# Fused four-layer cross-attention on one core: mean squares kept in PSUM, the last layer's bias in pieces, row maxima in another order and one unit earlier

## The chip, the cores and the metric

The kernel runs on 1 core of one Trainium2 chip. The time is device microseconds of one execution, the median of several runs. Lower is better. Engines: PE is TensorE, DVE is VectorE, ACT is ScalarE, POOL is GpSimd, SP issues the DMAs.

## The reference, cut to what matters

Four attention layers are applied in a row to `x` (4 batches x 512 tokens x 256 channels), each against the same context (4 x 1024 keys x 512 channels). Layers 0, 2 and 3 have 16 heads of 64 and add a bias of -20 on two or four key columns of masked tokens. Layer 1 normalizes `x` first (RMS norm) and has 16 query heads of 16 that share 4 key heads.

```python
# layers 0, 2, 3
q, k, v = x @ Wq, ctx @ Wk, ctx @ Wv                  # 16 heads of 64
logits = q k^T * 64**-0.5 + col_bias                  # 512 x 1024 per head
x = softmax(logits) v @ Wo + bo + x
# layer 1
inv = rsqrt(mean(x*x, axis=-1) + 1e-5); xn = x * inv * norm_w
q, k, v = xn @ wq, ctx @ wk, ctx @ wv                 # 16 query heads, 4 key heads, of 16
x = x + softmax(q k^T * 16**-0.5) v @ wo
```

## The kernel before, in words

**Items.** A wide layer is worked through as 32 items: 8 pairs of heads, and 4 batches for each. Layer 1 is 16 items: 4 groups of four heads, and 4 batches. So there are N = 112 items, numbered `p`; layer 1's are 32 to 47 (`G0` = 32, `G1` = 48), layer 2 starts at 48, layer 3 at 80. The kernel is a pipeline over slots `s`. In slot `s` PE computes the scores of item `s` (4 score blocks of two key tiles each), the row maxima of item `s+1`, the projections of keys and queries of item `s+2` and of values of `s+1`, and the second half of attention, the sums and the output projection of item `s-1`. Every engine has its instructions in an order written out by hand (`wide_slot`, `first_group_slot`, `group_slot`), the same sequence of names for all engines; semaphores with constants tie them together. f32 operands are split into two f16 halves, high and low (`k_h`, `k_l` and so on), and multiplied in three passes (`products`, L613).

**Row maxima.** `maxima(p, u)` has 8 units for a wide item: `t` is a block of 128 tokens, `half` a half of the 1024 keys. PE writes 2 heads x 512 scores to `ps_sm` (L684), which is a single buffer, and DVE adds the bias and takes the minimum of the negated sums in two custom instructions (L1293) with a read of the accumulator after each. A unit of the second half starts from the result of the first half (`nmx` is an operand), a unit of the first half from a constant. Two units go with each score block: one leads it and one trails it. Before the unit that trails, PE must wait until DVE is done with the one that leads. When all 8 units are done, ACT spreads the maxima (`columns_of_maxima`, L1037), PE transposes them (`rows_of_maxima`, L693) and DVE writes them to `ext_q` (`extra_rows`, L1314), from which PE adds them to the scores (L719).

**Two banks in turn.** Everything else that PE makes goes to `ps_j`, two banks used in turn in the order of `bank_users()`. `take` makes PE wait until the bank's last user has been read.

**RMS norm.** For the 4 batches (slots 30 to 33, `rms_batch`): ACT squares `x`, PE averages over channels with a matrix of 1/256 (`mean_squares`, L782), ACT copies the result to `v_rms` and takes exp(-0.5 ln), DVE refines it by one Newton step and multiplies `x` by it (`normed`, L1339 to L1344), POOL splits the product in `xh` and `xl` (`split_x`, L474 and L475), and PE projects the queries of layer 1 at the end of the slot (`late_queries`).

**Bias.** `bias_m` (4 token blocks x 1024 keys) holds the bias that DVE adds to the maxima. Eight matmuls (L790), one per token block and half, make it, each copied by ACT (L1065). Layer 3's are made in a row at the end of slot 78.

**Other names.** `second_half` (L1321) adds the two halves of attention in `o_un`; `sums_out` (ACT, L1016) and `reciprocal` (DVE, L1326, two of 256 columns) turn the row sums around; `normalize` (POOL, L523) multiplies; `output_hi` (ACT, L1044) and `output_lo` (POOL, L528) split the result for the output projection; POOL's `add` (L509) sums the exponentials over key tiles for the row sums.

## Time and profile before

| | |
|---|---|
| median of 3 runs | 3739.59 us (3733.17 to 3739.71) |
| the profiled execution | 3736.15 us, its span 3734.4 us |
| mean granted TensorE clock | 0.986 of full speed |
| PE busy | 3534.4 us, 95% |
| DVE, POOL, ACT busy | 66%, 54%, 46% |
| DMA | 39.44 MB, 11 GB/s over the span |

PE is busy nearly all the time. A slot of a wide layer takes 31.56 us in the middle of a layer; from 1027 to 1188 us, around the change to layer 1, slots are longer and the granted clock is lower. A row of the timeline reads: start, duration, engine, line, operation, output and inputs, shape, how many in a row, and in brackets how long the engine was idle before it and who ended that. Idle time matters where it is PE's.

### The profile page before, as it was taken

The page shows a single profiled execution, that of the slowest core. Times are in us where ns is not written, and L with a number is a line of the kernel's source. Part 1 is how long each engine was busy: PE and PEld are TensorE (multiplying, and loading weights), DVE is VectorE, ACT ScalarE, POOL GpSimd, SP SyncE. Part 2 cuts the span into 40 slices and gives each one's busy share as a digit, 9 for nine tenths or more (in the row PEclk, how much of TensorE's full clock was granted, in tenths as well). Part 3 has the DMA queues.
Part 4 walks back from the last instruction along what each step waited for, and adds up shares of the span by engine and source line. Part 5 has one row for each costly group of instructions (what it writes and reads, how often), then busy time and mean ns, then how long its engine had stood idle before and what let it go on. Part 6 is the DMA issues. An engine that isn't in the chain of part 4 may idle for free. (4 is left out here: it accounts for less than half of the span.)

```text
span 3734.4 us, 69744 instructions
## 1 busy us (share of the span) xinstructions
PE 3534.4 (95%) x27496; PEld 1552.8 (42%) x27496; DVE 2469.8 (66%) x4487; ACT 1704.6 (46%) x2146; POOL 2005.6 (54%) x968
## 2 busy tenths in 40 slices
PE   5999999999987888989999999999999999999997
PEld 2444444444432222224444444444444444444443
DVE  6666666666666788875666666666566666666664
ACT  3444444444444666664444444444444444444443
POOL 5755566666551000026556666656775555556666
PEclk8999999999998999999999999999999999999999
DMA  3000000000000000000000000000000000000000
GB/s 135 10 10 10 1 9 10 10 1 8 8 4 8 1 8 9 1 9 10 10 1 10 10 10 1 10 10 8 3 10 10 1 10 10 10 1 10 3 1 23
DMA packets 47503, 39.44 MB, mean 11 GB/s; under 512 B 2768, under 2 KB 40784, under 8 KB 47184
## 3 DMA queue, kind: packets, MB, share of 16 engines
q1 hardware_dynamic: 47184, 34.99, 3.0%
q8 instruction: 225, 3.69, 0.4%
q14 instruction: 94, 0.77, 0.1%
HBM read 32.88 MB, written 2.10 MB: 9 GB/s over the span
## 5 line engine op out<-in xcount | busy, mean ns | idle before, releaser
L509 POOL TENSOR_TENSOR acc<-acc,pt 128x1024 f32<-128x1024 f32 x576 | 1380.7, 2397 | 211.7 <-ACT pt L1011 170.5
L1011 ACT ACTIVATE pt<-ps_st 128x1024 f32<-128x1024 f32 x768 | 744.6, 1021 | 602.5 <-PE ps_st L719 602.5
L523 POOL TENSOR_TENSOR o_un<-o_un,rinv 128x512 f32<-128x512 f32 x112 | 142.7, 1274 | 1227.3 <-DVE rinv L1326 1227.3
L1293 DVE CUSTOM_DVE_ANT_0 ps_sm<-ps_sm,bias_m 128x512 f32<-128x512 f32 x760 | 510.9, 714 | 370.3 <-PE ps_sm L684 370.2
L761 PE MATMUL ps_j<-pt,v 128*64 128x512 f32 x3072 | 704.7, 601 | 2.0 <-ACT pt L1011 2.0
L1293 DVE CUSTOM_DVE_ANT_0 ps_sm<-ps_sm,bias_m,nmx 128x512 f32<-128x512 f32 x760 | 543.3, 756 | 69.3 <-PE ps_sm L684 60.0
L613 PE MATMUL ps_j<-w_h,ctx_h 128*128 128x128 f16 x3072 | 529.4, 220 | 0.5 <-DVE x L1334 0.5
L613 PE MATMUL ps_j<-w_h,ctx_l 128*128 128x128 f16 x3072 | 527.4, 220 | 0.0
L613 PE MATMUL ps_j<-w_l,ctx_h 128*128 128x128 f16 x3072 | 527.4, 220 | 0.0
L1326 DVE RECIPROCAL rinv<-rinv 128x256 f32<-128x256 f32 x224 | 391.3, 1748 | 64.1 <-ACT rinv L1016 63.8
L613 PE MATMUL ps_j<-ctx_h,w_h 128*128 128x512 f16 x896 | 342.0, 382 | 46.4 <-DVE o_un L1321 14.7
L761 PEld LDWEIGHTS ps_j<-pt,v 128*64 128x64 f32 x3072 | 204.2, 137 | 397.8 <-issue 394.3
L684 PE MATMUL ps_sm<-k_h,q_h 64*128 64x512 f16 x1528 | 300.7, 385 | 54.8 <-DVE nmx L1293 54.8
L613 PE MATMUL ps_j<-ctx_h,w_l 128*128 128x512 f16 x896 | 341.7, 381 | 0.0
L613 PE MATMUL ps_j<-ctx_l,w_h 128*128 128x512 f16 x896 | 341.7, 381 | 0.0
L1011 ACT ACTIVATE pt<-ps_sm 128x1024 f32<-128x1024 f32 x256 | 261.8, 1023 | 154.7 <-PE ps_sm L735 154.6
L1283 DVE TENSOR_REDUCE nmg<-ps_st 128x2 f32<-128x1024 f32 x248 | 295.8, 1212 | 48.1 <-PE ps_st L684 47.9
L613 PEld LDWEIGHTS ps_j<-w_h,ctx_h 128*128 128x128 f16 x3072 | 301.2, 98 | 44.8 <-issue 43.2
L1201 DVE SCALAR_TENSOR_TENSOR k_l<-ps_j,k_h 128x512 f16<-128x512 f32 x192 | 132.0, 688 | 280.5 <-ACT k_h L974 280.4
L613 PEld LDWEIGHTS ps_j<-w_l,ctx_h 128*128 128x128 f16 x3072 | 301.8, 98 | 0.0
L613 PEld LDWEIGHTS ps_j<-w_h,ctx_l 128*128 128x128 f16 x3072 | 301.7, 98 | 0.0
L509 POOL TENSOR_TENSOR acc<-pt 128x1024 f32<-128x1024 f32 x96 | 226.0, 2354 | 130.9 <-ACT pt L1011 130.9
(135 smaller groups left out, 4943.1 us busy)
## 6 DMA issues: line engine op xcount, KB each, us to landing
w_raw<-wk SPq DMA_DIRECT2D x28, 256.0 KB, 2.8
pt<-ctx_t SPq DMA_DIRECT2D x6, 1024.0 KB, 7.6
w_raw<-wv SPq DMA_DIRECT2D x24, 256.0 KB, 3.6
wo_raw<-wo SPq DMA_DIRECT2D x28, 128.0 KB, 2.0
w_raw<-wq SPq DMA_DIRECT2D x24, 128.0 KB, 2.8
x<-x_t SPq DMA_DIRECT2D x4, 512.0 KB, 8.4
acc<-ctx_t SPq DMA_DIRECT2D x2, 1024.0 KB, 8.2
out_t<-x SPq DMA_DIRECT2D x4, 512.0 KB, 2.8
```

Of the source, the lines that this page charges most:

```text
L509: G.tensor_tensor(total, first, pt[:, n % RING, :], ALU.add).then_inc(s_acc, 1)
L523: G.tensor_tensor(o, o, rinv[:], ALU.mult).then_inc(s_o, 1)
L613: done = MM(dst, l, r, start=first and i == 0, stop=last and i == n - 1)
L684: last = MM(dst[:, h, :], queries_in(p, tile)[d, t * P:(t + 1) * P], k_h[d, r, half * HALF:(half + 1) * HALF], start=True, stop=True)
L761: last = MM(dst[h * HD:(h + 1) * HD, :], values_of(p)[:, kt, h * HD:(h + 1) * HD], pt[:, (units(p) + kt) % RING, h * TQ:(h + 1) * TQ], sta ...
L1011: A(pt[:, n % RING, :], src.rearrange("p h q -> p (h q)"), ACT.Exp).then_inc(s_exp, 1)
L1201: return V.scalar_tensor_tensor(dst, src, scale, hi, ALU.mult, ALU.subtract)
L1283: V.tensor_reduce(nmg[:, half, t, 2 * tile:2 * tile + 2], src, AX_X, ALU.max, negate=True).then_inc(s_max, 1)
L1293: last = V.tensor_tensor_reduce(out=src[:, h, :], in0=src[:, h, :], in1=bias_m[:, t, half * HALF:(half + 1) * HALF], scale=-1.0, scalar=nm ...
L1326: V.reciprocal(r, r).then_inc(s_rinv, 1)
```

## The change

1. **Order and place of the maxima.** The units of a wide item come in the order of `piece`: (token block, half) = (0,0) (1,0) (0,1) (2,0) (1,1) (3,0) (2,1) (3,1). The first unit of item `s+2` is taken at the last of slot `s`'s eight places, so that the other seven of item `s+1` stand at the first seven places (`passes`, where `early` allows: items 1 to 31 and 50 to 111).
2. **Maxima out earlier.** ACT spreads the maxima before the exponentials 6 and 7 of the slot, PE transposes them in the middle of the second projection of values, so `extra_rows` stands on DVE ahead of the next slot.
3. **RMS norm.** For the first two batches the mean squares stay in their bank of `ps_j` and DVE works on them there; the other users of that stretch (`pvb`, `sum`, `k0`) share the other bank. The Newton step has three instructions in place of four. `normed` stands ahead of both reciprocals; ACT makes `xh` (`normed_hi`), POOL only `xl` (`normed_lo`). In slots 32 and 33 all of it moves a few steps later.
4. **Bias of layer 3.** Its eight matmuls are spread over slot 78 and the start of slot 79, one ahead of and one behind each score block.

```diff
+def last_bias(s, gap, after):
+    if after and gap < 0:
+        s, gap = s - 1, 3
+    return 16 + 2 * gap + after if s == STARTS[3] - 2 else None
+def piece(u):
+    return ((0, 0), (1, 0), (0, 1), (2, 0), (1, 1), (3, 0), (2, 1), (3, 1))[u]
+def early(p):
+    return p < N and not any(grouped(q) for q in (p - 2, p - 1, p)) and p >= 1
+def passes(s):
+    places = [[] for _ in range(8)]
+    p = s + 1
+    if 0 <= p < N:
+        for i, u in enumerate(range(1 if early(p) else 0, 8)):
+            places[i].append((p, u))
+    if early(s + 2):
+        places[7].append((s + 2, 0))
+    return places
...
@@ bank_users
+            bias(-1, 1)
             if rms_batch(s) is not None:
-                then("ms", rms_batch(s))
...
+                then("ms", rms_batch(s), 0)
+                then("pvb", s - 1, 1)
+                then("sum", s - 1, 1)
+                then("k0", s + 2, 1)
...
@@ POOL
-                if layer == GROUPED:
-                    pool.wait_ge(s_xn, b + 1)
-                    src = sq[:]
...
+            def normed_lo(b):
+                pool.wait_ge(s_xn_h, b + 1)
+                pool.wait_ge(s_q, queries(G0 - B + b + 1))
+                G.tensor_tensor(of_batch(xl, b), sq[:], of_batch(xh, b), ALU.subtract).then_inc(s_xs, 1)
@@ PE, take
+                    elif before == "ms" and m < 2:
+                        pe.wait_ge(s_xn, m + 1)
...
@@ PE, wide_slot
                 def score_block(i):
+                    if i and last_bias(s, i - 1, 0) is not None:
+                        bias_matrix(last_bias(s, i - 1, 0))
                     peak()
                     if now:
                         scores(s, i)
                     peak()
+                    if last_bias(s, i - 1, 1) is not None:
+                        bias_matrix(last_bias(s, i - 1, 1))
...
-                if nxt and has_values(s + 1):
+                if nxt and not grouped(s + 1):
+                    project_v(s + 1, 1, range(0, 2))
+                    rows_of_maxima(s + 1, 0)
+                    project_v(s + 1, 1, range(2, 4))
...
@@ PE, first_group_slot and group_slot
                 maxima(s, 9)
-                mean_squares(rms_batch(s))
+                attend(s - 1, 1)
                 maxima(s, 10)
-                attend(s - 1, 1)
...
-                    if i == 0 and s == G0 + 1:
+                    if i == 0 and first:
                         mean_squares(rms_batch(s))
...
-                    if i in (5, 6):
-                        if first:
-                            project_out(s - 1, i - 5)
+                    if i in (7, 8) and first:
+                        project_out(s - 1, i - 7)
...
+                    if i == 15 and first:
+                        mean_squares(rms_batch(s + 1))
@@ ACT
-                A(v_rms[:], bank("ms", b), ACT.Identity, bias=flags[:, FLAG_EPS:FLAG_EPS + 1]).then_inc(s_ms_sb, 1)
...
+                if b >= 2:
+                    A(v_rms[:], bank("ms", b), ACT.Copy).then_inc(s_ms_sb, 1)
...
+            def normed_hi(b):
+                act.wait_ge(s_xn, b + 1)
+                act.wait_ge(s_q, queries(G0 - B + b + 1))
+                A(of_batch(xh, b), sq[:], ACT.Copy).then_inc(s_xn_h, 1)
...
                     first_half_out(s)
+                    bias(2, 0)
+                if nxt and not grouped(s + 1):
+                    columns_of_maxima(s + 1)
+                if now:
                     exponentials(s, 6)
                     exponentials(s, 7)
-                if nxt and not grouped(s + 1):
-                    columns_of_maxima(s + 1)
...
@@ DVE
             def normed(b):
...
-                link(V.tensor_tensor(t_rms, y_rms[:], y_rms[:], ALU.mult))
-                link(V.tensor_tensor(t_rms, t_rms, v_rms[:], ALU.mult))
-                link(V.tensor_scalar(t_rms, t_rms, -0.5, 1.5, ALU.mult, ALU.add))
-                link(V.tensor_tensor(y_rms[:], t_rms, y_rms[:], ALU.mult))
+                ms = means_of(b)
+                link(V.scalar_tensor_tensor(ms, ms, EPS, y_rms[:], ALU.add, ALU.mult))
+                link(V.scalar_tensor_tensor(ms, ms, -0.5, y_rms[:], ALU.mult, ALU.mult))
+                link(V.scalar_tensor_tensor(ms, ms, 1.5, y_rms[:], ALU.add, ALU.mult))
...
-                if past:
+                if rms_batch(s) is not None:
+                    normed(rms_batch(s))
+                elif past:
                     reciprocal(s - 1, 0)
...
@@ DVE, group_slot
+                    if i in (4, 5) and first:
+                        reciprocal(s - 1, i - 4)
+                    if i == 6 and rms_batch(s) is not None:
                         normed(rms_batch(s))
```

**Order on PE at the end of a slot of a wide layer.** The rows are PE's around the transposition of the maxima (`nm_w`); `w_h`, `w_l` with `ctx_h`, `ctx_l` are the second projection of values, of which only the last rows stand here; `ps_sm` is the leading unit of maxima of the next slot. Before:

```order
L613 MATMUL ps_j<-w_h,ctx_h 128x128
L613 MATMUL ps_j<-w_l,ctx_h 128x128
L613 MATMUL ps_j<-w_h,ctx_l 128x128
L693 MATMUL ps_j<-ident_sb,nm_w 128x128 [waits s_x,s_nm16]
L693 MATMUL ps_j<-ident_sb,nm_w 128x128 x3
L684 MATMUL ps_sm<-k_h,q_h 128x512 [waits s_max,s_q_h,s_k_h]
```

Now, at the same place:

```order
L663 MATMUL ps_j<-w_l,ctx_h 128x128
L663 MATMUL ps_j<-w_h,ctx_l 128x128
L747 MATMUL ps_j<-ident_sb,nm_w 128x128 [waits s_x,s_nm16]
L747 MATMUL ps_j<-ident_sb,nm_w 128x128 x3
L663 MATMUL ps_j<-w_h,ctx_h 128x128
L663 MATMUL ps_j<-w_l,ctx_h 128x128
```

The transposition has moved ahead of the last 24 of the 48 matmuls of the projection; after these follows the next slot's leading unit.

**Order on ACT at the same place.** `o_un` is the first half of attention, `pt` the exponentials, `nm_w` the spread maxima, `v` the values. Before:

```order
L1021 ACTIVATE o_un<-ps_j 128x512 [waits s_o_l,s_pva]
L1011 ACTIVATE pt<-ps_st 128x1024 [waits s_acc,s_pva,s_st] x2
L1037 ACTIVATE nm_w<-nmx 128x512 [waits s_max,s_nm]
L995 ACTIVATE v<-ps_j 128x512 [waits s_pvb,s_v]
L1011 ACTIVATE pt<-ps_st 128x1024 [waits s_acc,s_pva,s_st] x2
```

Now:

```order
L1082 ACTIVATE o_un<-ps_j 128x512 [waits s_o_l,s_pva]
L1098 ACTIVATE nm_w<-nmx 128x512 [waits s_max,s_nm]
L1072 ACTIVATE pt<-ps_st 128x1024 [waits s_acc,s_pva,s_st] x2
L1056 ACTIVATE v<-ps_j 128x512 [waits s_pvb,s_v]
L1072 ACTIVATE pt<-ps_st 128x1024 [waits s_acc,s_pva,s_st] x2
```

The spread of the maxima now stands ahead of the last two exponentials of the slot, and waits for the maxima while these are queued behind it.

**Order on DVE in slot 30, the first with an RMS norm.** `rinv` is the reciprocal of the sums, `k_h` the low part of layer 1's keys, `sq`, `v_rms`, `y_rms` belong to the norm. Before:

```order
L1326 RECIPROCAL rinv<-rinv 128x256 [waits s_sum_sb]
L1339 TENSOR_TENSOR sq<-y_rms 128x512 [waits s_ms,s_rsqrt]
L1340 TENSOR_TENSOR sq<-sq,v_rms 128x512 [waits s_dve]
L1341 TENSOR_SCALAR sq<-sq 128x512 [waits s_dve]
L1342 TENSOR_TENSOR y_rms<-sq,y_rms 128x512 [waits s_dve]
L1344 TENSOR_TENSOR sq<-x,y_rms 128x512 [waits s_dve]
L1344 TENSOR_TENSOR sq<-x,y_rms 128x512
L1201 SCALAR_TENSOR_TENSOR k_h<-ps_j,k_l 128x512 [waits s_k_h]
```

Now, the norm first, and the reciprocals behind two units of maxima:

```order
L1405 TENSOR_TENSOR o_un<-ps_j,o_un 128x512 [waits s_pva_sb,s_pvb]
L1425 SCALAR_TENSOR_TENSOR ps_j<-ps_j,y_rms 128x512 [waits s_ms,s_rsqrt]
L1426 SCALAR_TENSOR_TENSOR ps_j<-ps_j,y_rms 128x512 [waits s_dve]
L1427 SCALAR_TENSOR_TENSOR ps_j<-ps_j,y_rms 128x512 [waits s_dve]
L1429 TENSOR_TENSOR sq<-x,ps_j 128x512 [waits s_dve]
L1429 TENSOR_TENSOR sq<-x,ps_j 128x512
...
L1410 RECIPROCAL rinv<-rinv 128x256 [waits s_sum_sb] x2
L1285 SCALAR_TENSOR_TENSOR k_h<-ps_j,k_l 128x512 [waits s_k_h]
```

The norm has moved from behind the second reciprocal to ahead of the first, and both reciprocals stand in one piece between the maxima of score block 1 and the second half of the keys.

## Rows read from the trace of the kernel before

**Rows 1.** The page: busy time of PE, its share, instructions.
```profile
PE 3534.4 (95%) x27496; PEld 1552.8 (42%) x27496; DVE 2469.8 (66%) x4487; ACT 1704.6 (46%) x2146; POOL 2005.6 (54%) x968
```

**Rows 2.** PE's waits, whole span: us in total, times, longest.
```profile
PE ps_sm L684 <- DVE nmx L1293: 54.8, 101, 7.5
```

**Rows 3.** PE's waits from 1750 to 2500 us.
```profile
PE ps_sm L684 <- DVE nmx L1293: 7.3, 24, 0.3
```

**Rows 4.** Timeline of PE around the end of slot 60, columns as above.
```profile
2131.36 0.39 PE L684 MATMUL ps_sm<-k_h,q_h 64*128 64x512 f16 x2
...
2133.35 0.39 PE L684 MATMUL ps_sm<-k_h,q_h 64*128 64x512 f16 x2
...
2136.68 0.39 PE L684 MATMUL ps_sm<-k_h,q_h 64*128 64x512 f16 x2
...
2139.00 0.39 PE L684 MATMUL ps_sm<-k_h,q_h 64*128 64x512 f16 x2 [0.30 <-DVE nmx L1293]
```

**Rows 5.** Timeline of DVE in the same stretch.
```profile
2131.80 0.70 DVE L1293 CUSTOM_DVE_ANT_0 ps_sm<-ps_sm,bias_m 128x512 f32<-128x512 f32 x1 [3.38 <-PE ps_sm L684]
...
2133.06 0.14 DVE L1293 DVE_READ_ACCUMULATOR2_ANT nmx<- 128x1 f32 x1
...
2133.78 0.76 DVE L1293 CUSTOM_DVE_ANT_0 ps_sm<-ps_sm,bias_m,nmx 128x512 f32<-128x512 f32 x1
...
2135.13 0.14 DVE L1293 DVE_READ_ACCUMULATOR2_ANT nmx<- 128x1 f32 x1
2136.79 0.75 DVE L1314 SCALAR_TENSOR_TENSOR ext_q<-ps_j,flags_sb,bias_q 128x512 f16<-128x512 f32 x1 [1.52 <-PE ps_j L693]
...
2138.71 0.14 DVE L1293 DVE_READ_ACCUMULATOR2_ANT nmx<- 128x1 f32 x1
```

**Rows 6.** Timeline of ACT in the same stretch.
```profile
2133.42 1.94 ACT L1011 ACTIVATE pt<-ps_st 128x1024 f32<-128x1024 f32 x2 [2.10 <-PE ps_st L719]
2135.64 0.63 ACT L1037 ACTIVATE nm_w<-nmx 128x512 f16<-128x512 f32 x1 [0.28 <-issue]
```

**Rows 7.** Timeline of PE in slot 30.
```profile
1032.62 1.03 PE L774 MATMUL ps_j<-acc,ones_sb 128*64 128x512 f32 x4
...
1053.54 0.61 PE L684 MATMUL ps_sm<-k_h,q_h 64*128 64x512 f16 x2 [7.48 <-DVE nmx L1293]
```

**Rows 8.** Timeline of DVE in slot 30.
```profile
1032.84 0.69 DVE L1321 TENSOR_TENSOR o_un<-ps_j,o_un 128x512 f32<-128x512 f32 x1 [4.02 <-PE ps_j L761]
1034.34 1.75 DVE L1326 RECIPROCAL rinv<-rinv 128x256 f32<-128x256 f32 x1 [0.81 <-ACT rinv L1016]
...
1041.79 0.63 DVE L1339 TENSOR_TENSOR sq<-y_rms 128x512 f32<-128x512 f32 x1
...
1044.12 2.45 DVE L1341 TENSOR_SCALAR sq<-sq 128x512 f32<-128x512 f32 x1
...
1048.16 3.31 DVE L1344 TENSOR_TENSOR sq<-x,y_rms 128x512 f32<-128x512 f32 x2
```

**Rows 9.** Timeline of DVE in the first slot of layer 1.
```profile
1125.49 0.43 DVE L1341 TENSOR_SCALAR sq<-sq 128x512 f32<-128x512 f32 x1
...
1136.33 0.19 DVE L1302 TENSOR_REDUCE nmx<-nmg 128x16 f32<-128x32 f32 x1
```

**Rows 10.** Timeline of ACT in slot 30.
```profile
1043.57 0.63 ACT L1044 ACTIVATE o_h<-o_un 128x512 f16<-128x512 f32 x1 [1.41 <-POOL o_un L523]
1044.15 0.78 ACT L971 ACTIVATE k_l<-ps_j,flags_sb 128x512 f16<-128x512 f32 x1
```

**Rows 11.** Timeline of POOL in slot 30.
```profile
1043.50 2.79 POOL L509 TENSOR_TENSOR acc<-acc,pt 128x1024 f32<-128x1024 f32 x1
```

**Rows 12.** Window 1052 to 1061: busy us of each engine (instructions), PEclk, DMA.
```profile
1052.00:1061.00 9.00, 7.46 (x22) 2.00 (x23) 3.48 (x10) 0.00 (x0) 8.77 (x4) 0.60 0.01 2
```

**Rows 13.** Timeline of PE at the end of slot 78.
```profile
2674.05 0.38 PE L790 MATMUL ps_j<-ext_k,bias_q 32*128 32x512 f16 x1
...
2679.07 0.61 PE L693 MATMUL ps_j<-ident_sb,nm_w 128*128 128x128 f16 x4
```

More of the change, by code:

```diff
@@ L111, in owner @@
     return p, n - units(p)
-def first_of_wide(p):
-    return p in (STARTS[i] for i in WIDE)
 def rms_batch(s):
@@ L210, in bank_users @@
             then("out0", s - 1, 1)
+        else:
+            then("ms", rms_batch(s + 1), 1)
         if s == G1 - 1:
@@ L378, in queries_in, with means_of @@
             return (q_l if tile else q_h)[:, p % 3, :]
+        def means_of(b):
+            return bank("ms", b) if b < 2 else v_rms[:]
         def of_batch(t, b):
@@ L548, in _ @@
                     add(s, 1)
[L549 to L550 removed]
+                if s == G0 + 1:
+                    normed_lo(rms_batch(s))
                 if past:
@@ L558, in _ @@
                     add(s, 3)
-                if rms_batch(s) is not None and not grouped(s):
-                    split_x(GROUPED, rms_batch(s))
                 if summing:
-                    for kt in range(4, KT):
+                    add(s, 4)
+                if rms_batch(s) is not None and s <= G0:
+                    normed_lo(rms_batch(s))
+                if summing:
+                    for kt in range(5, KT):
                         add(s, kt)
@@ L646, in project_v @@
                     wh, wl = w_h[:, set_of(p) % 2, WV0:], w_l[:, set_of(p) % 2, WV0:]
-                dst = take(f"v{half}", p)
-                for k in range(4):
+                if 0 in tiles:
+                    take(f"v{half}", p)
+                dst = bank(f"v{half}", p)
+                for k in tiles:
                     kt = slice((half * 4 + k) * P, (half * 4 + k + 1) * P)
@@ L1073, in wide_slot, with bias @@
                 now, nxt, far, past = 0 <= s < N, 0 <= s + 1 < N, 0 <= s + 2 < N, 0 <= s - 1 < N
+                def bias(gap, after):
+                    if last_bias(s, gap, after) is not None:
+                        bias_out(last_bias(s, gap, after))
                 def context(*parts):
@@ L1285, in maxima @@
                     return
-                t, half = u // 2, u % 2
-                if u == 0:
-                    reaches(dve, s_nm16, p)
+                t, half = piece(u)
+                if u in (0, 2):
+                    reaches(dve, s_nm16, p if u else p - early(p))
                 if half:
-                    dve.wait_ge(s_max, units(p) + u)
+                    dve.wait_ge(s_max, units(p) + [piece(i) for i in range(8)].index((t, 0)) + 1)
                 dve.wait_ge(s_bias_sb, 8 * WIDE.index(layer_of(p)) + u + 1)
```

139 lines of the change are left out of this document (75 added, 64 removed).

## Prediction

> **What bounds the kernel.** I read the page first, then PE's waits, then timelines. PE is busy for 95% of the span [rows 1], so time can come only from PE's waits, from the lower clock, or from fewer matmuls; the change adds and removes no matmul. The reader is to see in [rows 2] that the largest wait is for DVE's part of a unit of row maxima: 54.8 us in 101 waits. In 750 us in the middle of layers 2 and 3 there are 24 such waits of 0.3 us [rows 3], and 750 us are 24 slots: one in every slot. The rest of the 54.8 us lies in a few long waits, one of 7.48 us in slot 30 [rows 7].
>
> **The wait in every slot.** In [rows 4] the unit that leads a score block starts at 2131.36 and the one that trails it at 2133.35, 1.99 us later, with no wait. At the start of the next slot it is 2136.68 to 2139.00, 2.32 us: 0.33 more. [Rows 5] show why. DVE does `extra_rows` from 2136.79, released by PE's transposition, and begins the leading unit behind it; the unit ends at 2138.85, and PE starts 0.15 us later. Now PE transposes in the middle of the projection of values, some 1.6 us earlier (24 of the 48 matmuls that fill most of 2133.67 to 2136.36), so DVE is done with `extra_rows` before the leading unit arrives. 0.33 us go.
>
> What is late next? A unit of the first half takes DVE from 2131.80 to 2133.20, 1.40 us, and with 0.15 us to PE this is just the 1.99 us at which PE comes anyway: 2133.35. A unit of the second half takes 2133.78 to 2135.27, 1.49 us [rows 5]. Before, every leading unit was of the first half. In the new order those of score blocks 0, 1 and 2 still are, but block 3 is led by (3,1): its trailing unit waits 0.09 us. Net 0.24 us a slot. The slots with the wait are 1 to 29, 49 to 77 and 80 to 110, 89 in all: **21.4 us**.
>
> Two moves need cover. ACT spreads the maxima (0.63 us) ahead of exponentials 6 and 7 [rows 6], which start at 2133.42; the maxima are there at 2133.29, so the pair ends 0.6 us later, near 2136.0. PE's next scores overwrite that buffer from 2136.9 on (0.3 earlier now): 0.5 us of cover or more. And the transposition needs the spread maxima, near 2134.2, while PE comes to it after 2135. If the cover were gone, PE would wait for ACT in each slot. Moving one unit to the slot before moves work, it adds none; only in slot 48, where the last place has two units, does PE wait for a whole unit of DVE: 1.49 + 0.15 and the start, **2.0 us lost**. In slot -1 it has two as well, but slot 0 waits for DVE afterwards, and that wait shrinks: I count 0.6 us won.
>
> **Slot 30.** Before, the norm takes DVE from 1041.79 to 1051.47, 9.7 us [rows 8], and the unit of maxima behind it makes PE wait 7.48 us, until 1053.54 [rows 7]. Five of its six instructions would take some 0.7 us: the first does (0.63). The ones beside POOL's additions take 2.45 and 3.31 (for two); the same L1341 takes 0.43 in slot 32, where POOL does nothing [rows 8, 9, 11]. I bound the new norm by 3.5 us (five instructions of 0.7) and by 9.7, and take 3.5, as POOL waits for the reciprocals while it runs.
>
> The Trainium skill (SBUF — State Buffer, "Who interferes with whom") says that a VectorE instruction with two SBUF inputs or in a two-port mode contends with GpSimd for a shared pair of ports, and one with at most one SBUF input does not. The 2.45 against 0.43 us agrees. By that rule the new chain, with the mean squares in PSUM, would take 3.5 us even beside an addition, and the bound of 9.7 would not be met; the sum is the same.
>
> The chain then, all times as if in the old trace. The halves are added at 1032.84 for 0.69 [rows 8], 0.33 earlier now, to 1033.2. `sum` shares that bank now and can only start 0.15 later, at 1033.35, where it could have started at 1032.3; then ACT must read it (0.6) before `k0`: in all `k0` starts at 1035.2 instead of 1033.35. The norm runs from 1033.2 to 1036.7, in the gap of DVE that this opens; the first unit of block 1 comes 2.7 us after the start of `k0` (twelve matmuls of 0.22), at 1037.9. So the norm is hidden. But the reciprocals now stand behind the maxima of block 1: DVE is free for them at 1041.75, two take 3.4, one 1.75 [rows 8], POOL multiplies (1.4), ACT makes `o_h` (0.63) and only then the keys' high half (0.78) [rows 10], DVE its low half (0.68) and the leading unit of block 2 (1.4): 1050.05, PE at 1050.2. So a wait of some 2.6 us is left in place of 7.48, and its end comes 3.3 us earlier. After the old wait PE's clock is low: 0.60 over 1052 to 1061, with 7.46 us of matmuls [rows 12], which at full speed are 4.5: 3.0 us more to gain if the clock stays up after the shorter wait. That can't be read here; I count half. With 0.6 for the maxima that left slot 30 and for a bank freed earlier: 3.3 + 0.6 + 1.5 = **5.4 us**. The low half `xl` is ready by 1057, before PE asks for it near 1060.
>
> **Slot 31** has the same order, but one more instruction of 0.7 ahead of the norm, and the reductions wait for the queries' low half first: I take 1.5 less, **3.9 us**.
>
> **Start of layer 1.** DVE is the chain there, up to the minimum over both halves at 1136.33 [rows 9]. The norm (3.9 with its reads, no POOL beside it), two reciprocals (3.5) and PE's mean squares (2.0) leave it: 9.1 us earlier, allowing 0.3 for overlap. In slot 32, however, reciprocals and norm return on DVE between units 4 and 7, where it is still the chain: 3.5 + 3.6 come back, less 2.2 us in which it had waited for PE: 4.9. In slot 33 the norm now stands ahead of keys that PE waits for: 1.0. Net **3.2 us**.
>
> **Bias of layer 3.** From its first matmul at 2674.05 to the transposition at 2679.07 are 5.0 us [rows 13], and the low clock behind it adds 2.0 in a slot of 38.6. Spread out, each matmul costs 0.22 (1.8 for eight) and waits for the bank before it. I find 0.2 to 0.3 us for those that wait for DVE's low halves, and about 1.2, 1.0 and 0.8 where the next user waits for ACT's copy behind two exponentials (`pva`, `nm0`) or for the values: 4.1. So 5.9 for 7.0: **1.1 us**.
>
> **Sum.** 21.4 - 2.0 + 0.6 + 5.4 + 3.9 + 3.2 + 1.1 = 33.6 us. The profiled execution took 3736.15, 3.4 below the median of the runs shown: 3702.5 by the one, 3706.0 by the other. I take **3704 us**, own range 3693 to 3715.
>
> **The rivals.**
>
> *A. The waits around layer 1 only move* (0.20). Clock low again after waits of 2.6 us; the norm and the reciprocals, later, cost in slots 32 and 33 what was won ahead of them. For it: PE's clock is already low there, and `o_h` ahead of the keys on ACT is a new queue. Against it: 9.7 us on DVE really become 3.5. It leaves 21.1 us and nothing from the norm: 3716 us.
>
> *B. The norm's gain is not given back* (0.17). The clock stays up in slots 30 and 31 (1.5 + 1.0), and DVE takes norm and reciprocals in slot 32 where PE isn't waiting (4.9) and 33 (1.0). 8.4 us more: 3696 us.
>
> *C. The wait in each slot finds another engine* (0.08). PE's 1.99 us are exactly DVE's 1.40 + 0.15 from the start of DVE, so there is no slack, and block 3 or the spread maxima may take up the 0.24. Against it: nothing else on DVE precedes the unit. 21.4 less: 3725 us.
>
> *D. ACT holds PE, slower than before* (0.03). If exponentials 6 and 7 come more than 0.5 us later than I have them, PE's next scores wait in all slots. 33.6 us over 89 slots are 0.38 a slot: from exponentials 0.9 us later than reckoned the kernel is slower. At the whole 0.63 a slot 56 us are lost: 3760 us. Against it: the maxima that ACT waits for are done 0.13 us before it is free.
>
> The forecast has 0.52. Shared out, the range of 8 in 10 is 3686 to 3722: it takes in A and B, and leaves out C and D. What a measurement can tell from no change here is 0.2%, 7.5 us. Faster by more: all but D and the tail of C: 0.94; within: 0.03; slower: 0.03.
>
> **What would show it.** In the new profile: no wait for `nmx` at the start of a slot, trailing units at 1.99 us in blocks 0 to 2 and at 2.08 in block 3, `nm_w` ahead of the exponentials, a slot near 31.3 us. In slot 30 the norm on DVE as five instructions near 0.7 us, a wait of PE for DVE of 2 to 3 us at block 2, the granted clock after it. In slot 32 reductions, reciprocals and norm without a gap on DVE. In slot 78 waits of PE at `pva` and at the transposition. Wrong would be: slots still of 31.5 us, PE waiting for ACT in ordinary slots, or a wait over 5 us in slots 30 and 31.

## The result and the profile after

The changed kernel takes **3688.49 us** (median of 4 runs, 3687.80 to 3690.56), the kernel before beside it 3736.38 (4 runs). The ratio is 0.9874, 95% interval 0.9857 to 0.9891: 47.9 us, or 1.3%, faster. The forecast was 3704 us, a gain of 33.6, with a range from 3686 to 3722. So direction and range held, and so did the mechanism of the largest term, but 14 us more came than the sum had, and the narrower range of 3693 to 3715 was missed. The profiled execution's span went from 3734.4 to 3686.0 us. One of the four executions of `dve_late` below took 10273.54 us at a granted clock of 0.333 and is left out of its figures.

On the page, PE's busy time is nearly what it was [rows 1]; the 48 us came out of its waits.

```profile
PE 3531.1 (96%) x27496; PEld 1554.9 (42%) x27496; DVE 2406.0 (65%) x4483; ACT 1696.2 (46%) x2148; POOL 1995.9 (54%) x964
```

PE's waits over the whole span, kernel after (total us, times, longest), answering to [rows 2]:

```profile
PE ps_sm L738 <- DVE nmx L1377: 23.0, 12, 5.7
...
PE ps_j L663 <- POOL o_l L574: 16.0, 4, 7.3
```

The same view of 1750 to 2500 us, answering to [rows 3], has one line left:

```profile
PE ps_j L663 <- DVE o_un L1405: 0.6, 1, 0.6
```

From 101 waits for the maxima 12 are left. But the reader should put a second row of before beside these. It was in the same answer as [rows 2], and the prediction passed it over:

```profile
PE ps_j L613 <- DVE o_un L1321: 14.7, 29, 1.2
```

After, waits of this kind are down to four (0.6 in slots 9 and 53 each, 0.9 in slots 30 and 31 each). These waits are most of what the forecast missed.

**An ordinary slot after** (end of a slot on PE; start us, us, then in brackets the idle time ahead and who ended it), answering to [rows 4]:

```profile
2096.39 0.39 PE L738 MATMUL ps_sm<-k_h,q_h 64*128 64x512 f16 x2
...
2098.46 0.39 PE L738 MATMUL ps_sm<-k_h,q_h 64*128 64x512 f16 x2
...
2100.14 0.39 PE L747 MATMUL ps_j<-ident_sb,nm_w 128*128 128x128 f16 x4
```

On DVE and ACT in the same stretch, answering to [rows 5, 6]:

```profile
2100.56 0.75 DVE L1398 SCALAR_TENSOR_TENSOR ext_q<-ps_j,flags_sb,bias_q 128x512 f16<-128x512 f32 x1 [0.26 <-PE ps_j L747]
2102.23 0.70 DVE L1377 CUSTOM_DVE_ANT_0 ps_sm<-ps_sm,bias_m 128x512 f32<-128x512 f32 x1 [0.92 <-PE ps_sm L738]
```
```profile
2098.41 0.63 ACT L1098 ACTIVATE nm_w<-nmx 128x512 f16<-128x512 f32 x1 [2.05 <-DVE nmx L1377]
2098.94 1.92 ACT L1072 ACTIVATE pt<-ps_st 128x1024 f32<-128x1024 f32 x2
```

`ext_q` is done at 2101.31, 0.92 us before DVE is handed the leading unit of the next slot: DVE now waits for PE there, and not PE for DVE. The trailing unit of block 3 comes 2.07 us after the leading one (2098.46 against 2096.39), as forecast (2.08). The maxima are spread ahead of the exponentials; ACT waits 2.05 us for them, as it waited 2.10 us for PE's scores there before [rows 6], and PE waits for nobody.

To compare slot by slot I take the time from a slot's first exponential on ACT to the next slot's; the last row ends with the last exponential, and what follows it took 19.1 us before and 20.2 after. The sums, us against the profiled execution of before (a minus is faster):

| Part | before | after, change | forecast |
|---|---|---|---|
| before slot 0, and slot 0 | 103.7 | -5.2 | -0.6 |
| slots 1-29 | 922.9 | -12.6 | -7.0 |
| slots 30-33 | 200.9 | -12.5 | -12.5 |
| slots 34-47 | 468.4 | -1.1 | 0 |
| slot 48 | 27.7 | +3.9 | +2.0 |
| slots 49-77 | 921.2 | -12.4 | -7.0 |
| slots 78, 79 | 70.1 | -1.3 | -1.1 |
| slots 80-109 | 948.7 | -9.3 | -7.2 |
| slots 110, 111 | 51.7 | +1.0 | -0.2 |

A plain slot went from 31.56 to 31.31 us, in every one of them: 0.25, forecast 0.24. What the forecast lacks lies in slots 5, 13, 17, 21 and so on, one in four, which went from 31.84 to 31.31, and in slots 9 to 12 and 53 to 56, from between 32.22 and 32.76 to 31.31 to 31.92. The first and the last row hold more than the change: executions of one order differ there. From slot 111's first exponential to the end of the span `before` took 41.2 us, and `norm_only` and `wo_late`, which have the old order too, 44.0, like the changed kernel.

### The profile page after: what moved, and what is told of

It reads as the page before. It is cut to its first block, busy times and chain, and to the rows that moved or that the text cites. A ratio compares the mean times of both kernels' runs of the same rounds, so it can differ in the third digit from the quotient of the medians.

```text
span 3686.0 us, 69837 instructions
## 1 busy us (share of the span) xinstructions
PE 3531.1 (96%) x27496; PEld 1554.9 (42%) x27496; DVE 2406.0 (65%) x4483; ACT 1696.2 (46%) x2148; POOL 1995.9 (54%) x964
## 4 chain that ended last, share of the span: by engine, by line
PE 90%; DVE 4%; issue 3%; ACT 2%; POOL 1%; DMA 0%; POOLq 0%; ACTq 0%; DVEq 0%
PE ps_j L663 39%; PE ps_j L815 18%; PE ps_st L767 13%; PE ps_sm L738 7%; PE ps_st L773 3%; PE ps_j L802 3%; PE ps_j L828 2%; PE ps_st L738 1%; PE ps_sm L789 1%; PE ps_j L747 1%; ACT pt L1072 1%; DVE nmg L1367 1%; ACT k_l L1032 1%; DVE k_h L1285 1%; DVE ps_sm L1377 0%
## 5 line engine op out<-in xcount | busy, mean ns | idle before, releaser
L767 PE MATMUL ps_st<-q_h,k_h 64*128 64x512 f16 x1536 | 291.4, 376 | 2.0 <-ACT pt L1072 2.0
```

Source lines behind the costliest of these rows:

```text
L767: MM(ps_st[:, side, h, :], k[d, r, keys], q[d, r, :], start=n == 0, stop=False)
```

## The experiments

All ratios are against the kernel before, run on the same chip.

**The small instruction ahead of o_un.** In one slot in four, DVE makes the low half of Wo (`wo_l`, 128x256) between the trailing unit and `o_un`. Slot 61 before, DVE and then POOL:

```profile
2108.93 2.62 DVE L1201 SCALAR_TENSOR_TENSOR wo_l<-wo_raw,wo_h 128x256 f16<-128x256 f32 x1
2111.47 0.68 DVE L1321 TENSOR_TENSOR o_un<-ps_j,o_un 128x512 f32<-128x512 f32 x1
```
```profile
2108.91 2.35 POOL L509 TENSOR_TENSOR acc<-pt 128x1024 f32<-128x1024 f32 x1 [1.39 <-ACT pt L1011]
```

Slot 5 after:

```profile
225.45 0.42 DVE L1285 SCALAR_TENSOR_TENSOR wo_l<-wo_raw,wo_h 128x256 f16<-128x256 f32 x1
227.69 0.69 DVE L1405 TENSOR_TENSOR o_un<-ps_j,o_un 128x512 f32<-128x512 f32 x1 [1.83 <-PE ps_j L815]
```
```profile
225.76 2.36 POOL L555 TENSOR_TENSOR acc<-pt 128x1024 f32<-128x1024 f32 x1 [1.00 <-ACT pt L1072]
```

Before, POOL's addition starts 0.02 us ahead of DVE's instruction, and this takes 2.62 us; after, DVE starts 0.31 us ahead of POOL, and it takes 0.42. The trailing unit used to be 0.33 us late while the exponential that releases POOL was not.

The token rows (slots 8 to 12 and 52 to 56) are a second case of it, at the same place on DVE. Slot 10, before and then after:

```profile
391.00 3.41 DVE L1252 SCALAR_TENSOR_TENSOR sq<-iota_sb,tok_f,sq 128x1024 f16<-128x1024 f16 x1
```
```profile
382.62 1.28 DVE L1336 SCALAR_TENSOR_TENSOR sq<-iota_sb,tok_f,sq 128x1024 f16<-128x1024 f16 x1
```

POOL's addition starts at 390.98 there, 0.02 us ahead, and at 382.93, 0.31 us behind. Two kernels test this.

The first, `dve_late`, is the changed kernel with POOL's start put ahead of DVE's again:

```diff
+                    dve.wait_ge(s_exp, units(s) + 2)
+                    V.tensor_copy(tok_f[:, 0, 0:1], tok_f[:, 0, 0:1])
                     wo_lo(set_of(s - 1))
```

> The changed kernel; ahead of the low half of Wo, DVE now waits for exponential 1 (the same event that releases POOL's first addition) and does one 128x1 copy, so that POOL's addition starts first. Nothing is moved or added otherwise. The theory (whoever starts first keeps the shared SBUF port for its whole instruction): the 128x256 instruction takes 2.6 us again instead of 0.42, o_un is late, and PE waits 0.6 to 0.7 us for it in 20 to 22 slots, as in slot 9 where one such case is left (0.64): 3688.5 + 14 = 3702 us. Rival (the instruction is faster for another reason than the order, for example because it has less to wait for from ACT): it stays at 0.42 to 0.5 us, DVE is ready 0.5 us before attend ends, and the time stays within 1 us of 3688.5.

Measured 3702.60 us (3 runs, 3700.56 to 3702.80; ratio 0.9920, 0.9903 to 0.9936): the gain of the change less 14.1 us. Its row of `wo_l` (min/median/max ns) and PE's wait, then slot 5:

```profile
L1285 DVE SCALAR_TENSOR_TENSOR wo_l<-wo_raw,wo_h x28: 411/2610/2617, 100.4 to 3594.2; 128x256 f16<-128x256 f32 x28
```
```profile
PE ps_j L663 <- DVE o_un L1405: 14.2, 21, 1.0
```
```profile
225.58 2.36 POOL L555 TENSOR_TENSOR acc<-pt 128x1024 f32<-128x1024 f32 x1 [0.99 <-ACT pt L1072]
```
```profile
225.61 2.61 DVE L1285 SCALAR_TENSOR_TENSOR wo_l<-wo_raw,wo_h 128x256 f16<-128x256 f32 x1
228.14 0.68 DVE L1405 TENSOR_TENSOR o_un<-ps_j,o_un 128x512 f32<-128x512 f32 x1
```

The same instruction, started 0.03 us behind POOL's and not 0.31 ahead, takes 2.2 us longer and ends 0.28 us after it. The start order decides. The copy and the wait cannot cost this by themselves: they start `wo_l` 0.16 us later, and in the changed kernel DVE had 1.83 us of idle time between `wo_l` and `o_un`. Nineteen slots went from 31.31 to 31.92, and 9 and 53 from 31.92 to 32.32. That is 0.61 us in a plain slot, where the same blocking cost 0.28 in the kernel before: PE was 0.33 us late there anyway. The token rows have no added wait in this kernel, still take 1.28 us in slot 10, and their slots did not get longer.

The second, `wo_late`, is the kernel before, with `wo_lo` and `token_rows` of slots 8 to 12 and 52 to 56 taken out of that place:

```diff
-                if past and (s - 1) % B == 0:
-                    wo_lo(set_of(s - 1))
-                for w, start in ((1, 8), (2, G1 + 4)):
-                    ...
                 if past and not grouped(s - 1):
                     second_half(s - 1)
...
                     keys_lo(s + 2, 1)
+                if past and (s - 1) % B == 0:
+                    wo_lo(set_of(s - 1))
+                for w, start in ((1, 8), (2, G1 + 4)):
+                    ...
```

> The kernel before with one thing moved on DVE: the low half of Wo and the token rows, which stand ahead of the sum of the halves (o_un) in 24 and 10 slots, go behind the low half of the keys in the gap after block 1, where DVE has more than 3 us to spare. The theory: PE's 29 waits for o_un (14.7 us) come from these instructions, which take 2.6 us beside POOL's first addition; all 29 go, nothing takes their place, the 0.30 us wait for maxima stays in every slot: 3736.4 - 14.7 = 3722 us. Rival: the waits come from the trailing unit of maxima that was 0.33 us late, the instruction between is innocent: o_un is then still late in those slots and the time stays at 3736. Rival 2: in the new place the instruction holds up the maxima of block 2 or POOL's additions: gain under 8 us, 3728 or more.

Measured 3729.72 us (10 runs; ratio 0.9988, 0.9979 to 0.9997), 3.1 us less than before took in this comparison, where 14.7 was expected. All 29 waits for `o_un` went, and slots 5, 13, 17 fell to 31.56 like their neighbours; `wo_l` takes 0.41 to 0.42 us in its new place. But eight slots have a new wait for the maxima, since the token rows now stand ahead of block 2:

```profile
PE ps_sm L684 <- DVE nmx L1293: 62.2, 109, 7.5
```

That is 7.4 us more than in [rows 2], half of the 14.7. Slots 10 to 12 fell by 0.27 only, and slots 9 and 53 rose by 0.56. So the second rival held for the token rows, the theory for `wo_l`. By the profiled executions the ordinary slots gained 6.4 us, twice what the medians show.

**The parts of the order.** `natural` keeps the early unit, but gives back the old order of halves:

```diff
-    return ((0, 0), (1, 0), (0, 1), (2, 0), (1, 1), (3, 0), (2, 1), (3, 1))[u]
+    return u // 2, u % 2
```

> The changed kernel with the units of maxima in their old order, both halves of a tile in a row; one unit is still done a place ahead. Now every score block is led by a second half, whose DVE time is 1.49 us instead of 1.40. The theory (forecast's figures: PE comes 1.99 us after the leading unit, a second half is back after 2.08): 0.09 us of wait in each of four blocks instead of in one, 0.27 a slot more, 89 slots: 3688.5 + 24 = 3712 us, slots of 31.58; part of slot starts comes late too, so the o_un waits of 0.3 us may come back (+6). Rival: the 0.09 is hidden in blocks 0 to 2, the order does nothing: 3688 us.

Measured 3712.77 us (4 runs; ratio 0.9938, 0.9922 to 0.9955), 24.3 over the changed kernel, as expected to 0.3 us. A plain slot takes 31.57 us, so all four blocks now pay 0.09 us. The view of waits does not show it (its gap in the records is 0.06 us); it stands in the distance between starts, 2.07 us in each block. The o_un waits did not come back.

`no_shift` takes the early unit away and keeps the two other moves:

```diff
-    return p < N and not any(grouped(q) for q in (p - 2, p - 1, p)) and p >= 1
+    return False
```

> The changed kernel without the unit that is done one place ahead: the last unit of a slot's eight stays in the last place, but ACT still spreads the maxima ahead of exponentials 6 and 7, and PE still transposes in the middle of the projection of values; the order of halves stays. The theory: the early unit is what makes the other two moves possible: ACT now waits for the last unit, some 2 us after exponential 6 could start, PE waits for the transposition and then for the exponentials of the last block: 0.3 to 1.5 us a slot more than 31.3, 3715 to 3820 us, as slow as before or slower. Rival: moving the transposition alone wins the 0.3 us, the early unit is not needed: 3688 to 3695 us.

Measured 3799.28 us (4 runs; ratio 1.0173, 1.0158 to 1.0189), 1.7% slower than before. From 1750 to 2500 us:

```profile
PE ps_j L747 <- ACT nm_w L1098: 19.8, 23, 0.9
```

A plain slot takes 32.52 us, 1.21 more than after. Of this, 0.86 is the wait above; and with eight units in their own slot blocks 1 to 3 are each led by a second half (2.07 us to the trailing unit, and 1.99 in block 0), two more than after, 0.09 each. So the 0.25 us need the order of halves and the early unit together; the earlier transposition without the early unit loses. The early unit with the transposition in its old place was not run.

**The norm.** `norm_only` is the kernel before with the norm's part alone (its diff is that of the change without `piece`, `early`, the moved transposition, the spread maxima and the bias in pieces); `no_norm` is the changed kernel with the old norm in its old places.

> The kernel before with the new norm alone: mean squares in PSUM, five DVE instructions, the two reciprocals behind the norm, the high half on ACT, the low half on POOL; the order of the maxima, the place of the transposition and the bias of layer 3 stay as they were. The theory: the norm is worth by itself what slots 30 to 33 gained together in the changed kernel, 12.5 us, and nothing elsewhere: 3736.4 - 12.5 = 3724 us, and the 0.3 us wait at the start of each slot and the waits for o_un stay. Rival 1: part of the 12.5 us came from the new order of the maxima (PE comes to slot 30 0.33 us earlier, and slots 30 to 32 have no wait at their starts): some 8 us, 3728. Rival 2: the norm also freed something in the ordinary slots: below 3718.

> The changed kernel with its norm taken back to the old one (mean squares copied to SBUF, reciprocals ahead of the norm); everything else as changed. The theory says that the two parts add up: 3688.5 + 12.5 = 3701 us, a gain of 35.4 over before, more than the 27.9 us that the forecast had for these parts (21.4 - 2.0 + 0.6 + 1.1, and the rest of the missed o_un waits). PE waits some 7.5 us for maxima in slot 30, as before. Rival: the norm's gain needs the earlier maxima, or the other way round: then this kernel is 3695 or less, or 3708 or more.

Measured: `norm_only` 3722.15 us (10 runs; ratio 0.9972, 0.9962 to 0.9981), `no_norm` 3702.97 (4 runs; ratio 0.9923, 0.9908 to 0.9938). In `no_norm` slots 30 to 33 are within 0.3 us of before and all other parts as after, but for 1.0 us in slots 34 to 47; in `norm_only` slots 30 to 33 gain 10.3 us and the ordinary slots nothing. The two savings, 10.7 and 29.8 us by the medians, fall 7.4 short of 47.9. Of this, 3.6 is that before took 3732.8 us in this comparison and 3736.4 in that of the result; the intervals of the ratios are wider than the rest. In the profiled executions the parts add up in the ordinary slots to 0.1 us. Elsewhere they differ both ways: slots 34 to 47 lack 4.7 us (3.4 of it in slots 40 and 44 of `norm_only`, at a granted clock of 0.91 and 0.95), slots 30 to 33 lack 1.9, which stays open, the last two lack 1.7, and the stretch up to the end of slot 0 has 4.4 too much, since it was longest in the execution of before.

`sbuf_norm` asks what of it is PSUM and what is the place. It is the changed kernel with the mean squares of batches 0 and 1 copied to SBUF again:

```diff
-            return bank("ms", b) if b < 2 else v_rms[:]
+            return v_rms[:]
...
-                if b >= 2:
-                    A(v_rms[:], bank("ms", b), ACT.Copy).then_inc(s_ms_sb, 1)
-                    act.wait_ge(s_ms_sb, b - 1)
+                A(v_rms[:], bank("ms", b), ACT.Copy).then_inc(s_ms_sb, 1)
+                act.wait_ge(s_ms_sb, b + 1)
```

> The changed kernel with the mean squares of the first two batches copied to SBUF by ACT again, so that the first three of DVE's five instructions read and write SBUF; their place, ahead of the reciprocals, stays. Theory 1 (the place does it): POOL does nothing from 1013.17 to 1027.26 in slot 30, because it waits for the reciprocals, so the three instructions take 0.4 to 0.9 us each in SBUF as well; one copy of 0.6 us is added on ACT, partly hidden: 3688.5 + 0 to 1.2 = 3689 us. Theory 2 (PSUM does it, since with one SBUF input DVE does not contend with POOL): the instructions take 1.5 to 3.3 us each as in the kernel before, the norm ends 3 to 6 us later in both slots, and part of the old wait is back: 3694 us or more.

Measured 3690.29 us (4 runs, 3687.77 to 3692.29; ratio 0.9886, 0.9869 to 0.9902), not to be told from 3688.49. Slot 30 takes 39.51 us in both. DVE in its slot 30, and below it the changed kernel's:

```profile
1015.42 0.69 DVE L1422 SCALAR_TENSOR_TENSOR v_rms<-v_rms,y_rms 128x512 f32<-128x512 f32 x1 [0.32 <-ACT y_rms L1116]
1016.15 0.69 DVE L1423 SCALAR_TENSOR_TENSOR v_rms<-v_rms,y_rms 128x512 f32<-128x512 f32 x1
```
```profile
1015.28 0.69 DVE L1425 SCALAR_TENSOR_TENSOR ps_j<-ps_j,y_rms 128x512 f32<-128x512 f32 x1
...
1017.47 1.28 DVE L1429 TENSOR_TENSOR sq<-x,ps_j 128x512 f32<-128x512 f32 x2
```

POOL in the changed kernel's slot 30 says why:

```profile
1010.82 2.35 POOL L555 TENSOR_TENSOR acc<-pt 128x1024 f32<-128x1024 f32 x1 [0.99 <-ACT pt L1072]
1027.26 1.26 POOL L569 TENSOR_TENSOR o_un<-o_un,rinv 128x512 f32<-128x512 f32 x1 [14.08 <-DVE rinv L1410]
```

For 14 us POOL does nothing, because it waits for the reciprocals, which stand behind the norm. The norm is short for its place; PSUM buys nothing here. What the Newton step's three instructions in place of four and the high half on ACT are worth by themselves was not run.

**The reciprocals.** `recip_first`, slots 30 and 31:

```diff
-                elif past:
+                if past:
                     reciprocal(s - 1, 0)
...
-                if rms_batch(s) is not None:
-                    reciprocal(s - 1, 0)
                 if past:
                     reciprocal(s - 1, 1)
```

> The changed kernel; in slots 30 and 31 DVE does the first reciprocal right behind the norm, where it waits for PE anyway, instead of behind the maxima of block 1. The theory (the waits of 2.29 us at block 2 of slot 30 and 1.89 us in slot 31 end with the chain reciprocals, POOL's product, o_h and the keys on ACT, DVE): both fall to 0.5 us or less, and slot 31's clock may stay up (it fell for one stretch after that wait, some 2 us): 3688.5 - 3.4 = 3685 us, down to 3683 with the clock. In slot 31 the first unit of block 1 may be 0.6 us late. Rival: the chain runs by way of POOL's additions or the keys' projection: the waits stay, 3688 us.

Measured 3686.13 us (4 runs, 3684.66 to 3687.04; ratio 0.9870, 0.9855 to 0.9885). The two waits in the changed kernel, answering to [rows 7], and then PE's waits here in slots 30 and 31 (total, times, longest):

```profile
1032.04 0.39 PE L738 MATMUL ps_sm<-k_h,q_h 64*128 64x512 f16 x2 [2.29 <-DVE nmx L1377]
...
1071.80 0.39 PE L738 MATMUL ps_sm<-k_h,q_l 64*128 64x512 f16 x2 [1.89 <-DVE nmg L1367]
```
```profile
PE ps_sm L738 <- DVE nmg L1367: 1.7, 3, 0.9
...
PE ps_sm L738 <- DVE nmx L1377: 1.1, 1, 1.1
```

Slot 30 fell by 1.23 us and slot 31 by 2.40: the chain is the one named, but the two waits kept 1.1 and 0.9 us, where 0.5 or less was expected. How much of the 2.40 is the move is less sure: four more executions with the order of the changed kernel in slot 31 (`dve_late`, `natural`, `sbuf_norm`, `bias_together`) took 55.4 to 57.05 us there, against its 57.04 and 54.64 here.

**The bias of layer 3.** `bias_together` puts the eight matmuls back in a row at the end of slot 78, with the transposition of that slot behind them:

```diff
-    return 16 + 2 * gap + after if s == STARTS[3] - 2 else None
+    return None
...
-                if s == -2:
+                if s in (-2, STARTS[3] - 2):
                     for i in range(8):
-                        bias_matrix(i)
+                        bias_matrix(8 * WIDE.index(layer_of(s + 2)) + i)
```

> The changed kernel with the eight bias matmuls of layer 3 and their copies together again at the end of slot 78, and the transposition of that slot behind them. The theory: the pieces are worth what slots 78 and 79 show between the two traces, 1.3 us (forecast 1.1): slot 78 back near 38.6, 3689.8 us. Rival: with the early unit, the copies behind the last exponentials now hold up more than before: slot 78 above 40, 3692 or more.

Measured 3688.95 us (4 runs; ratio 0.9885, 0.9871 to 0.9900), no difference. Slots 78 and 79 take 69.04 us, against 68.83 in pieces. PE over slot 78, in pieces and then together (us, busy us of PE, PEld, DVE, ACT, POOL with instructions, PEclk, DMA):

```profile
2605.00:2642.00 37.00, 33.80 (x261) 15.28 (x259) 19.25 (x41) 16.66 (x24) 28.99 (x15) 1.00 0.01 1
```
```profile
2606.00:2643.00 37.00, 35.12 (x260) 15.49 (x256) 19.15 (x41) 17.43 (x25) 32.34 (x16) 0.96 0.01 1
```

In pieces PE is idle longer (3.2 us of the 37 against 1.9) at the full clock; together it waits less and the clock falls to 0.96. The two cancel but for 0.2 us.

**Versions that go on from it.** `combo` has `recip_first`, and three moves:

```diff
+                    held.extend(here[1:])
+                    for p, u in here[:1]:
                         maxima(p, u)
...
                     project_v(s + 1, 1, range(0, 2))
+                    for p, u in held:
+                        maxima(p, u)
                     rows_of_maxima(s + 1, 0)
```

on PE for the places with two units; `wo_lo` alone behind `keys_lo(s + 2, 1)`; and the last third of `weights_lo` for layer 1 behind `extra_rows`.

> The changed kernel with four small moves: the first reciprocal right behind the norm (slots 30, 31); in slots -1 and 48, which have two units at their last place, PE issues the second one two tiles into the projection of values instead of at once; the low half of Wo goes behind the low half of the keys, after block 1; of the three instructions for the low half of layer 1's weights the last goes behind the extra rows of slot 28. The theory: 3.4 for the first, 1.67 us of wait in slot 48 and about as much again from its clock (0.95), 0.64 + 0.05 us in slots 9 and 53 each, 1.6 us in slot 28: 3688.5 - 3.4 - 3 - 1.3 - 1.5 = 3679 us. Rival: the wait of slot 48 only moves to the transposition (DVE does the extra rows behind the second unit): 3682. Second rival: the waits that are left are worth nothing, 3687.

Measured 3684.59 us (4 runs; ratio 0.9869, 0.9854 to 0.9883). Slot 48 fell from 31.60 to 28.95, slots 9 and 53 to 31.32. Slots 28 and 29 came to the same sum (64.20): the wait only moved. By the end of slot 0 2.4 us were lost, with the unit held back in slot -1. So 5.6 us of the expected gain did not come.

`final` keeps what paid: no split of `weights_lo`, and the unit held back in slot 48 alone. `final_32` adds:

```diff
-                    if i in (4, 5) and first:
-                        reciprocal(s - 1, i - 4)
+                    if i in (3, 4) and first:
+                        reciprocal(s - 1, i - 3)
```

> The changed kernel with the three moves that paid in the last run: first reciprocal behind the norm, the second unit of slot 48 (not that of slot -1) two tiles into the projection, the low half of Wo behind the low half of the keys. By slots: 30 and 31 -3.6, 48 -2.65, 9 and 53 -1.2, nothing else: 3688.5 - 7.5 = 3681 us. Rival: a shift of clock at the end takes 1.7 of it back: 3683.

> The kernel above; in slot 32 the two reciprocals stand one unit of maxima earlier on DVE (behind units 3 and 4 instead of 4 and 5). The theory of slot 32: PE's wait of 4.1 us ends with the chain reciprocals, POOL's product, o_h, o_l, and what the changed kernel lost there (6.3 us against before) is this chain behind DVE's maxima, which before was finished in slot 31's end. The wait should shrink by 1.7 to 2.8 us, and units 4 and 5 come 1.7 later on DVE: net 0 to 2 us faster than the kernel above, 3679 to 3681. Rival: DVE's maxima are the chain all through slot 32, and any order of the same instructions gives the same time: wait shorter, slot as long.

Measured: `final` **3681.41 us** (4 runs, 3680.70 to 3682.06; ratio 0.9864, 0.9849 to 0.9879), `final_32` 3680.43 (4 runs, 3679.88 to 3685.21; ratio 0.9866, 0.9849 to 0.9882). By the medians they are 7 and 8 us under the changed kernel. The kernel before took 3732.16 us in this comparison, so by the ratios it is 3.7 and 3.0 us, with intervals that overlap; slot by slot the profiled execution of `final` gains 6.4 us in slots 1 to 77, where its moves are. From each other the two cannot be told. PE's waits in slot 32, changed kernel and then `final_32`:

```profile
1114.61 0.61 PE L663 MATMUL ps_j<-o_h,wo_h 128*128 128x512 f16 x1 [4.11 <-POOL o_l L574]
```
```profile
1106.09 0.61 PE L738 MATMUL ps_st<-k_h,q_l 64*128 64x512 f16 x2 [1.53 <-DVE nmg L1374]
...
1108.16 0.61 PE L663 MATMUL ps_j<-o_h,wo_h 128*128 128x512 f16 x1 [1.03 <-POOL o_l L574]
...
1113.31 0.58 PE L663 MATMUL ps_j<-o_h,wo_h 128*128 128x512 f16 x1 [2.72 <-DVE x L1425]
```

The wait of 4.11 shrank to 1.03 and others took its place: over the whole slot PE waits 15.0 us in the changed kernel and 14.8 in `final_32`, and the slot is as long as after (51.44 against 51.41). The rival held. In the first 14 us of slot 32 DVE does not pause (its first idle time in the changed kernel is 0.49 us, ahead of 1119.78), and the order of the same instructions on it does not shorten that. In `final`, from which it differs by this move alone, slot 32 took 52.34 us and slot 31 0.47 less; the sum of the two is 0.4 us apart.

## Why the prediction was right, and by what it was off

The direction came from a mechanism that was forecast. That the time still fell within 3686 to 3722 us owes something to luck: the lower end had been drawn for rival B, which did not occur (slots 32 and 33 gave back 6.8 us), and a term that the sum did not have filled the room.

- **The wait in every slot: right in mechanism and size.** Forecast 0.33 less 0.09, measured 0.25, with the trailing unit of block 3 at 2.07 us; `natural` shows that the 0.09 is real and paid per block, `no_shift` that the early unit is needed. Rivals C and D (another engine takes the wait) fell: in a plain slot PE waits for nobody.
- **The term that was missing: 12.3 us.** The prediction took one row of PE's waits as the whole effect and did not ask what stands behind the late unit on DVE. In slots 1 to 29, 49 to 77 and 80 to 109 the gain is 34.3 us, of which 0.25 x 88 = 22.0 is the plain wait; the other 12.3 lie where PE waited for `o_un`: about 5 us in the slots with `wo_l` and 7.1 in those with token rows alone. `dve_late` brought 12.3 us back as well, but that the two are equal is chance: its 12.3 are 0.61 us in each slot with `wo_l`, where `before` lost 0.28, and nothing in the slots of the token rows. So for `wo_l` an experiment shows the cause; for the token rows it is read from the rows (3.41 us against 1.28 by the same turn of the start order), and no run turned it back. The prediction had the mechanism in hand (2.45 against 0.43 us for one instruction in [rows 8, 9]), but applied it to the norm alone.
- **Slots 30 to 33: 12.5 forecast, 12.5 measured, shares other than thought.** Slot 30 gave 6.1 us (forecast 5.4): the norm is five instructions near 0.7 where [rows 8] had 2.45 and 3.31, the wait at block 2 is 2.29 (forecast 2.6) for the 7.48 of [rows 7], and the clock in the 9 us behind that wait (1032.04 to 1041.04) is 1.00 where [rows 12] had 0.60. Slots 31 to 33 together gave 6.4 (forecast 7.1), as 13.2 gained in slot 31 (3.9 + 9.1 forecast, since the 9.1 us of the start of layer 1 lie ahead of slot 32's first exponential) and 6.3 and 0.5 lost in slots 32 and 33 (4.9 and 1.0 forecast): reciprocals and norm, late, cost 0.9 more than was said. The match of the sum is closer than executions repeat: in `dve_late`, `natural`, `sbuf_norm` and `bias_together`, which keep that part, slots 30 to 33 gained 11.1 to 13.7 us. The clock that stayed up in slot 30 fell in slot 31 after a wait of 1.89 us, shorter than slot 30's (0.79 over 1071.8 to 1080). That half of the clock would come back was luck: one slot kept it, one did not, and in `bias_together` slot 30, with the same instructions, took 40.93 us at a clock of 0.96.
- **The reason given beside it, mean squares in PSUM, was wrong.** The 3.5 us did not depend on it (`sbuf_norm`). The forecast's other ground, that POOL waits for the reciprocals meanwhile, is the whole of it. The Trainium skill (SBUF — State Buffer, "Who interferes with whom") says that a DVE instruction with at most one SBUF input, outside the two-port modes, does not contend with GpSimd; with POOL idle during the norm, these rows can't show that.
- **Start: 0.6 forecast, 5.2 measured, but the size is not shown.** Up to the end of slot 0 `before` took 103.7 us, but the two other kernels with the old order took 99.6 (`norm_only`) and 100.8 (`wo_late`), against 98.5 after: the gain is 1.1 to 5.2 us by the execution taken. Two things set the changed kernel apart from all three. Its slot 0 takes 26.9 us at a clock of 1.00, theirs 31.0 at 0.95. And DVE's `context_lo`, the row below, takes 2.76 us, in theirs 3.44 to 3.78. That it starts at 68.44 and not at 71.40 is no effect of the change: in `norm_only` it starts at 67.28. Why slot 0 is shorter is open.

```profile
71.40 3.62 DVE L1209 TENSOR_TENSOR ctx_l<-pt,ctx_h 128x2048 f16<-128x2048 f32 x1
```
```profile
68.44 2.76 DVE L1293 TENSOR_TENSOR ctx_l<-pt,ctx_h 128x2048 f16<-128x2048 f32 x1
```

- **Slot 48: 2.0 forecast, 3.9 measured.** The wait is 1.67 us, as thought, but the clock behind it is 0.72 for 6 us, 1.7 us more. Some 0.5 us is the moved unit itself (an estimate: PE's busy time in the slot rose by 2.15 us, of which the clock is 1.7). `combo` takes most of the wait and the low clock away (2.65 us).
- **Bias: 1.1 forecast, 1.3 measured, for the wrong reason.** `bias_together` shows that the pieces are worth 0.2; the other 1.1 us lies with what moved along with them (the wait of 0.30 at the start of both slots, the maxima spread earlier). Two plain slots' worth of it is 0.5. No run told the rest apart.

## What to carry to other kernels

When a unit on a tight engine gets earlier, list every instruction behind it on its engine up to the next wait, and see what each overlaps with on its neighbours: its duration may depend on a start order that you are about to change. And go through all rows of the bound engine's waits, not the largest alone; a wait of 0.3 us that only one slot in four has is a second mechanism. A wait taken out is not worth its length alone: waits of 1.9 and 1.7 us had some 1.4 us of low clock behind them in slots 31 and 48 (what `recip_first` and `combo` won there beyond the wait), a wait of 2.3 us in slot 30 had none in that execution. And when an experiment gives back just the number that was missing, look at which slots gave it back.

## What the runs showed of the hardware

Beside POOL's addition (128x1024, two inputs from SBUF, 2.35 us) `wo_l` takes 0.42 us or 2.6, by a start 0.31 us ahead of POOL's or 0.02 behind, and then ends 0.28 us after POOL's instruction. It goes the other way too: where DVE's token row started 0.31 us ahead (slot 10, 382.62), POOL's addition took 3.19 us. The blocking is to be seen in the changed kernel's slot 32 as well, where POOL's `o_l` runs to 1114.55 (POOL, then DVE):

```profile
1113.01 1.54 POOL L574 TENSOR_TENSOR o_l<-o_un,o_h 128x512 f16<-128x512 f32 x1 [0.74 <-ACT o_h L1105]
```
```profile
1112.85 0.69 DVE L1426 SCALAR_TENSOR_TENSOR v_rms<-v_rms,y_rms 128x512 f32<-128x512 f32 x1
1113.58 1.52 DVE L1427 SCALAR_TENSOR_TENSOR v_rms<-v_rms,y_rms 128x512 f32<-128x512 f32 x1
```

L1426, which started first, keeps its 0.69 us beside `o_l`; L1427, of the same shape, waits for POOL to end. By the Trainium skill (the same section), whoever issues first holds the shared pair for the whole instruction and the other fully blocks. Beside POOL's additions this case agrees, with 0.42 and 2.62 us. Beside its other instruction it does not: in slot 1 of the changed kernel `wo_l` starts 0.73 us behind a POOL TENSOR_SCALAR and is done 1.45 us before its end:

```profile
99.47 2.78 POOL L515 TENSOR_SCALAR xh<-x 128x1024 f16<-128x1024 f32 x1
```
```profile
100.20 0.60 DVE L1285 SCALAR_TENSOR_TENSOR wo_l<-wo_raw,wo_h 128x256 f16<-128x256 f32 x1
```

The two of slot 81 do the same. So here the start order decides against POOL's two-input instructions; why the one-input one does not block is open.
